# Attention stack on one core: projection weights, Wo and the key cache read already transposed

## What is computed

```python
q = einsum('bsd,ed->bse', x, Wq)   # 32 heads of 128
k = einsum('bsd,ed->bse', x, Wk)   # 8 heads of 128
v = einsum('bsd,ed->bse', x, Wv)   # 8 heads of 128
q, k = rope(rmsnorm(q, q_norm_w)), rope(rmsnorm(k, k_norm_w))
k_all = concat(k_cache[block_table], k)   # 512 cached keys + 32 new ones
v_all = concat(v_cache[block_table], v)
probs = softmax(where(valid, q @ k_all.T * scale, -1e30))
out = x + einsum('bse,de->bsd', probs @ v_all, Wo)
```

## Time and profile before

| | |
|---|---|
| median of 3 runs | 1507.56 us (1506.31 to 1509.15) |
| span of the profiled execution | 1508.6 us |
| TensorE busy | 1439.5 us, 95% |
| VectorE busy | 979.2 us, 65% |
| ScalarE busy | 813.0 us, 54% |
| GpSimd busy | 736.6 us, 49% |
| layers, projection, attention, output begin at about | 0, 203, 558, 1300 us |
| DMA | 275 MB, 182 GB/s over the span |

### The profile page before, as it was taken

How to read it: one execution, slowest core, us unless ns; L and a number is a source line. 1 busy time by engine, 2 the same in 40 slices (tenths; PEclk the granted TensorE clock), 3 DMA queues, 4 the chain that set the end, 5 groups by cost and what they waited for, 6 DMA issues and landing times. The chain is left out here.

```text
span 1508.6 us, 32191 instructions
## 1 busy us (share of the span) xinstructions
PE 1439.5 (95%) x9308; PEld 1265.8 (84%) x9308; DVE 979.2 (65%) x2630; ACT 813.0 (54%) x1930; POOL 736.6 (49%) x738
## 2 busy tenths in 40 slices
PE   5988989999999958999999999999999999789999
PEld 4766879999999947999999999998999999678887
DVE  4669966666666547777777777777777777542221
ACT  2156734444444336777777777776777777431111
POOL 2004027787777766665656666664656665000000
PEclk9999999999999978999999999999999999899999
DMA  6310034555554579988888888897988885443332
GB/s 187 135 50 18 22 127 112 171 143 170 170 170 136 162 216 277 250 239 241 257 244 235 251 249 238 244 253 202 258 234 243 259 238 152 144 156 122 124 117 76
DMA packets 273737, 275.13 MB, mean 182 GB/s; under 512 B 61461, under 2 KB 231701, under 8 KB 273686
## 3 DMA queue, kind: packets, MB, share of 16 engines
q1 hardware_dynamic: 263638, 249.24, 57.1%
q0 software_dynamic: 9472, 25.21, 6.2%
q10 hardware_dynamic: 576, 0.05, 0.0%
HBM read 219.88 MB, written 54.53 MB: 182 GB/s over the span
## 5 line engine op out<-in xcount | busy, mean ns | idle before, releaser
L1212 DVE CUSTOM_DVE_ANT_1 att_neg<-att_mask,att_ps 128x576 f32<-128x576 f32 x256 | 193.0, 754 | 154.8 <-PE att_ps L95 154.8
L1105 POOL TENSOR_TENSOR att_k_lo<-att_kT,att_k_hi 128x544 fp32r<-128x544 f32 x128 | 173.4, 1355 | 143.2 <-ACT att_k_hi L1314 143.2
L1105 POOL TENSOR_TENSOR att_k_lo<-all_room_a,att_k_hi 128x544 fp32r<-128x544 f32 x128 | 174.2, 1362 | 136.4 <-ACT att_k_hi L1314 136.4
L1299 ACT ACTIVATE att_prob<-att_neg,att_nmax 128x544 f32<-128x544 f32 x256 | 191.6, 748 | 29.0 <-DVE att_nmax L1212 6.3
L1305 ACT ACTIVATE att_pT<-att_pb 128x256 f32<-128x256 f32 x256 | 98.1, 383 | 183.7 <-PE att_pb L1145 183.7
L93 PE MATMUL att_ps<-att_k_hi,att_q_lo 128*128 128x288 f32 (+1 forms) x512 | 171.3, 335 | 12.0 <-POOL att_k_lo L1105 11.9
L93 PE MATMUL prj_ps<-prj_wt_hi,early_xT_lo 128*128 128x512 f32 (+1 forms) x512 | 178.4, 349 | 2.2 <-DVE prj_wt_lo L892 2.2
L94 PE MATMUL prj_ps<-prj_wt_lo,early_xT_hi 128*128 128x512 f32 (+1 forms) x512 | 173.5, 339 | 0.0
L95 PE MATMUL prj_ps<-prj_wt_hi,early_xT_hi 128*128 128x512 f32 (+1 forms) x512 | 172.9, 338 | 0.0
L94 PE MATMUL att_ps<-att_k_lo,att_q_hi 128*128 128x288 f32 (+1 forms) x512 | 148.9, 291 | 0.0
L95 PE MATMUL att_ps<-att_k_hi,att_q_hi 128*128 128x288 f32 (+1 forms) x512 | 148.9, 291 | 0.0
(11 more groups left out here) (169 smaller groups left out, 3860.9 us busy)
## 6 DMA issues: line engine op xcount, KB each, us to landing
all_room_a<-kt_scratch SPq DMA_DIRECT2D x256, 128.0 KB, 3.7
att_kT<-kt_scratch SPq DMA_DIRECT2D x256, 128.0 KB, 3.4
all_room_b<-in_L_cond_v_cache SPq DMA_DIRECT2D x160, 128.0 KB, 3.0
att_vc<-in_L_cond_v_cache SPq DMA_DIRECT2D x160, 128.0 KB, 3.1
q_scratch<-prj_qst SPq DMA_DIRECT2D x64, 256.0 KB, 2.2
o_scratch<-att_ost SPq DMA_DIRECT2D x32, 512.0 KB, 4.5
out_o_n<-o_scratch SPq DMA_DIRECT2D x32, 512.0 KB, 3.4
all_room_b<-in_L_cond_v_cache POOLq DMA_DIRECT2D x96, 128.0 KB, 3.9
```

The lines of the kernel that those rows point to most:

```text
L1105: g.tensor_tensor(k_lo[j % SPLITS][:], kT[j // HK % 2][:, :, j % HK, :], f32(k_hi[j % SPLITS][:]), ALU.subtract).then_inc(k_split, 1)
L1212: v.tensor_tensor_reduce(halves[0], halves[1], ps[j % 2][:, :, 0:KA], 1.0, 3.0e38, ALU.add, ALU.min, nmax[j % 2][:]).then_inc(maxed, 1)
L1299: act.activation(prob[j % 2][:], neg[j % 2][:, 0:KEYS], ACT.Exp, bias=nmax[j % 2][:, 0:1], scale=-1.0, accum_out=total[j % 2][:]).then_inc ...
```

## The change

The host now hands over three arrays in another layout (`laid_out`): `wqkv_t`, for each key head the rows 0 to 511 by its 768 columns of Wq, Wk and Wv; `wo_t`, Wo transposed; `k_cache_t`, each page as [128, 8 heads, 32 positions]. The kernel drops all transposes of weights, of Wo and of the key cache, the `pw` banks, the stores to and the existence of `kt_d`, and the loads of `kn`. The hi and lo splits read the loaded weights from SBUF. In the projection they are now four pieces per head, 768 columns each, in bodies t = 0, 2, 4, 6; TensorE has a new wait ahead of `multiply(j + 2)` at t = TT - 2 = 6. `load_head` is one DMA in place of three. In the output stage two chunks (1024 columns) are split at once, and SP's waits ahead of a slice's load are on the splits.

```diff
-def load_head(eng, inp, c, tile, sem):
-
-    for name, rows, o in zip(("L3_cond_Wq", "L3_cond_Wk", "L3_cond_Wv"), (QW, D, D), (0, REP, REP + 1)):
-        src = inp[name].rearrange("(c o p) i -> c p o i", p=P, o=rows // P)[bass.ds(c, 1)]
-        eng.dma_start(tile[:, o:o + rows // P, :], src.rearrange("a p o i -> (a p) o i")).then_inc(sem, 16)
...
+def load_head(eng, inp, c, tile, sem):
+
+    src = inp["wqkv_t"][bass.ds(c, 1)].rearrange("a (k p) e -> p (a k) e", p=P)
+    eng.dma_start(tile, src).then_inc(sem, 16)
...
+        def split_at(t, last_head):
+
+            return t % 2 == 0 and not last_head
...
                     if t == 0 and not tail:
 
-                        sp.wait_ge(job_t, job_of(c, 0))
-                        load_w(c + 2, slot)
+                        sp.wait_ge(w_hi_done, (c + 1) * KC)
+                        sp.wait_ge(w_lo_done, (c + 1) * KC)
+                        load_head(sp, inp, c + 2, wn[slot][:], w_in[slot])
...
-                pe.wait_ge(w_in[0], 48)
-                for g in range(WJ):
-                    weight_job(g, 0, first_banks[g])
-                pe.wait_ge(job_dve, WJ)
+                pe.wait_ge(w_lo_done, KC)
                 multiply(0)
                 multiply(1)
...
-                        if t == 0 and not last_head:
-                            pe.wait_ge(w_in[1 - slot], (it + 1 + slot) * 48)
-                        if not cache_step(t, last_head):
-                            weight_job(t, 1 - slot, pw[:, t % 2])
-                        else:
-                            pe.wait_ge(kn_in[t % 2], (c + 1) * 16)
-                            cache_job(t % 2)
                     if not (tail and j >= UNROLL - 2):
 
                         pe.wait_ge(roped, n + 1)
                         pe.wait_ge(v_staged, n + 1)
+                        if t == TT - 2:
+                            pe.wait_ge(w_lo_done, (c + 2) * KC)
                         multiply(j + 2)
...
+                    if split_at(t, tail and slot == 1):
+                        if t == 0:
+                            act.wait_ge(w_in[1 - slot], (it + 1 + slot) * 16)
+                        k = t // 2
+                        act.activation(wt_hi[1 - slot][:, k, :], wn[1 - slot][:, k, :], ACT.Copy).then_inc(w_hi_done, 1)
...
+                def split_lo(k, slot, done):
+
+                    dve.wait_ge(w_hi_done, done)
+                    v.tensor_tensor(wt_lo[slot][:, k, :], wn[slot][:, k, :], f32(wt_hi[slot][:, k, :]),
+                                    ALU.subtract).then_inc(w_lo_done, 1)
...
+                    if split_at(t, tail and slot == 1):
+                        k = t // 2
+                        split_lo(k, 1 - slot, (c + 1) * KC + k + 1)
                     if not (tail and j >= UNROLL - 2):
                         rope(j + 2, n + 2)
...
-    eng.dma_start(tile[:], inp["L3_cond_Wo"][:, s * w:(s + 1) * w].rearrange("(o p) e -> p o e", p=P)).then_inc(sem, 16)
+    eng.dma_start(tile[:], inp["wo_t"][s * w:(s + 1) * w].rearrange("(c p) o -> p c o", p=P)).then_inc(sem, 16)
...
                 for s in range(2, SL):
-                    sp.wait_ge(w_turned, (s - 1) * CS)
+                    sp.wait_ge(w_hi, (s - 1) * CS // WG)
+                    sp.wait_ge(w_lo, (s - 1) * CS // WG)
...
-                turn(0)
                 for i in range(UNROLL):
-                    if i + 1 < Q:
-                        turn(i + 1)
                     body(0, i, False)
...
-                    for c in range(q * CQ, (q + 1) * CQ):
-                        act.wait_ge(w_turned, c + 1)
-                        act.activation(wt_hi[:, c, :], pw[c % 4][:], ACT.Copy).then_inc(w_hi, 1)
+                    for c in range(q * CQ, (q + 1) * CQ, WG):
+                        s = c // CS
+                        act.wait_ge(w_in[s % 2], 16 * (s // 2 + 1))
+                        act.activation(wt_hi[:, c:c + WG, :], wn[s % 2][:, c % CS:c % CS + WG, :], ACT.Copy).then_inc(w_hi, 1)
...
-                    for c in range(q * CQ, (q + 1) * CQ):
-                        dve.wait_ge(w_hi, c + 1)
-                        v.tensor_tensor(wt_lo[:, c, :], pw[c % 4][:], f32(wt_hi[:, c, :]), ALU.subtract).then_inc(w_lo, 1)
+                    for c in range(q * CQ, (q + 1) * CQ, WG):
+                        s = c // CS
+                        dve.wait_ge(w_hi, c // WG + 1)
+                        v.tensor_tensor(wt_lo[:, c:c + WG, :], wn[s % 2][:, c % CS:c % CS + WG, :],
+                                        f32(wt_hi[:, c:c + WG, :]), ALU.subtract).then_inc(w_lo, 1)
```

More of the change, by code:

```diff
@@ L645, in stage_project @@
         pt = m.psum("pt", [P, 2 * BANK])
-        pw = m.psum("pw", [P, 2, BANK])
-        first_banks = [pw[:, 0], pw[:, 1]] + [x[:, i * BANK:(i + 1) * BANK] for x in (pt, ps[1]) for i in range(2)]
         w_in = [w_in0, m.sem("w_in1")]
[L651 to L654, removed]
+        w_hi_done = m.sem("w_hi_done")
+        w_lo_done = m.sem("w_lo_done")
         mm_done = m.sem("mm_done")
@@ L1037, in load_keys @@
             for j, page in enumerate(pages):
[L1038 removed]
+                load_key_page(eng, inp, kT[slot], j, page, kq_in[slot])
         def load_new_values(eng, b, slot):
@@ L1366, in stage_output @@
         x3, y = ([room[:, (2 * a + i) * H:(2 * a + i + 1) * H] for i in range(2)] for a in range(2))
-        pw = [m.psum(f"pw{i}", [P, BANK]) for i in range(4)]
         py = [m.psum(f"py{i}", [P, BANK]) for i in range(2)]
-        w_turned = m.sem("w_turned")
         w_hi = m.sem("w_hi")
@@ L1427, in _ @@
             def _(pe):
-                def turn(q):
-                    for c in range(q * CQ, (q + 1) * CQ):
-                        s = c // CS
-                        if c % CS == 0:
-                            pe.wait_ge(w_in[s % 2], 16 * (s // 2 + 1))
-                        if c >= 4:
-                            pe.wait_ge(w_lo, c - 3)
-                        for o in range(KC):
-                            t = pe.transpose(pw[c % 4][:, o * P:(o + 1) * P], wn[s % 2][:, o, c % CS * P:(c % CS + 1) * P],
-                                             ident[:])
-                        t.then_inc(w_turned, 1)
                 def body(it, i, tail):
@@ L1573, in inverse_frequencies, with laid_out @@
     return (np.float32(1.0) / np.power(np.float32(THETA), np.arange(0, D, 2, dtype=np.float32) / np.float32(D))).astype(np.float32)
+def laid_out(inputs):
+    a = {n: np.asarray(inputs[n]) for n in INPUTS}
+    heads = lambda n: a[n].reshape(HK, -1, H)
+    rows = np.concatenate([heads("L3_cond_Wq"), heads("L3_cond_Wk"), heads("L3_cond_Wv")], axis=1)
+    for n in ("L3_cond_Wq", "L3_cond_Wk", "L3_cond_Wv"):
+        del a[n]
+    a["wqkv_t"] = rows.transpose(0, 2, 1)
+    a["wo_t"] = a.pop("L3_cond_Wo").T
+    a["k_cache_t"] = a.pop("L3_cond_k_cache").transpose(0, 3, 2, 1)
+    a["rope_inv_freq"] = inverse_frequencies()
+    return {n: np.ascontiguousarray(x) for n, x in a.items()}
 def kernel(**inputs):
@@ L1581 @@
     arrays, args = {}, {}
-    for name in INPUTS + ["rope_inv_freq"]:
-        a = inverse_frequencies() if name == "rope_inv_freq" else np.ascontiguousarray(inputs[name])
+    for name, a in laid_out(inputs).items():
         arrays[f"in_{name}"] = a
```

122 lines of the change are left out of this document (23 added, 99 removed).

## The result

| | before | after |
|---|---|---|
| median of 4 runs | 1506.96 us (1506.31 to 1509.15) | 1519.52 us (1515.15 to 1521.20) |
| span of the profiled execution | 1508.6 us | 1513.5 us |
| TensorE busy | 1439.5 us | 1406.3 us |
| GpSimd busy | 736.6 us | 754.9 us |
| DMA | 275 MB | 258 MB |

The ratio of the times is 1.0078, with a 95% interval of 1.0061 to 1.0095: the change makes the kernel slower, by 12.6 us between the medians and 11.8 by the ratio. All ratios leave out one run that took 3484 us, of the kernel with the key cache's part alone. The forecast was 6.0 slower, 1513.6; the range of 1499 to 1526 holds the time. TensorE is busy 33 us less and the kernel is later all the same, so the loss is idle time and a low clock (a matmul's record is also longer while the clock is low, so part of that loss stands in the busy time).

A forecast was written before the change was run, and what follows sets the result against it. TensorE was taken to bound the projection, attention and the end of the output stage. Removed jobs -30.3, stalls +29.6, clock +11.2, start -0.4 and output -4.1 gave +6.0, so 1513.6 us, range 1499 to 1526.

The forecast's parts named there:

- The ruler: Projection: distances between five-transpose groups (L822) price removed work at 16.4 us for weight jobs and 13.9 for cache jobs.
- The estimate of 123 us: Projection: 448 removed transposes at about 275 ns each; the prediction used the steps' 30.3 us instead.
- The stall: Projection, body 6: TensorE waits for the last lo piece until S + 4.8, S starting body 5's transposes; 4.2 us, seven heads, 29.6.
- VectorE held by GpSimd: Last lo subtraction in the projection waits for GpSimd's addition (L946); stall 4.2 us with this, 3.3 without.
- the three earlier pieces: Projection, bodies 0, 2, 4: each delays GpSimd by about 0.9 us, costed at zero; up to 10 us without cover.
- The clock: Projection: granted clock falls after each of seven stalls, costing 1.6 us each, 11.2 us; bounds zero and 23 us.
- rival (b): Projection stalls: clock stays low twice as long, as at 1041; 11.8 us more, 1525 us; chance 0.10.
- The start: Start of the projection: first splits take 4.6 us in place of 5.0 before TensorE's first matmul, a gain of 0.4.
- The output stage: Output stage: unit 2 starts 5.5 us earlier, less 1.5 for low clock; a gain of 4, bounds 0 and 7.
- Attention: Attention keeps its instructions and reads key pages from another tensor in the same pieces; effect put at zero.
- The sum: Whole kernel: -30.3 + 29.6 + 11.2 - 0.4 - 4.1 = +6.0 us, added to the median for 1513.6 us.
- rival (f): Projection: no stall, for instance because pieces are ready earlier; the change gives its full 34.8 us, 1472.8; chance 0.04.

## Why the prediction held, and where it was off

**The ruler: right.** Reading the cost of a job from the distance of the L822 groups gave 16.4 and 13.9 us; the runs have 16.2 and 14.0. The estimate of 123 us from the Trainium skill's figure for one transpose ("TensorE: Matmul & The Clock Gate", section "Part 4: PE-mode transpose") is refuted. The skill states that figure for bf16, and the record here has 272 ns in float32; but the transposes of weights and cache in the loop were worth 30.2 us, and the output stage as a whole 4.9.

**The stall: right, in size and in its parts.** Laid out was S + 4.8, measured is S + 4.67; 4.2 us a head, 29.6 in all, against 29.6 by the steps with the clock up. That the tenths agree is luck: the layout itself gives 4.26 a head, the rounded 4.2 gives 29.4. VectorE held by GpSimd costs 0.84 us of it, against 0.9. The Trainium skill, "SBUF — State Buffer", section "SBUF: two separate sides", calls it an exclusive lock held for the whole instruction; the trace agrees, with 0.95 us for the subtraction alone and 1.78 beside GpSimd's addition. Putting the three earlier pieces at zero was right too: no step up to body 61 but the seven is longer than 4.77 us.

**The clock: right that it falls, wrong in size.** This is the term that was mis-sized: "Matmul work in 3.4 us at half speed loses 1.7, less if part of the low stretch falls in the idle time. I take 1.6 us each." Measured are 2.1 a head by the kernel with work in the stall, 14.4 to 14.9 in all against 11.2. In the trace of after the low stretch lasts 6.8 us at five of the seven stalls, where it begins 1.2 to 1.9 us before TensorE does, and 3.4 at two, where it begins 1.3 us behind it. So 5.0 to 5.6 us of it lie on matmuls in five heads and 3.4 in two, and the steps are 2.2 to 2.6 and 1.6 us longer than the 8.99 with the clock up: the 1.6 was right for the short stretch, and the caveat on the idle time was right, but most stretches are the long one. The row that showed this length was there, 6.6 us at 0.52 behind 1041.45; it went into rival (b) as a case for all seven heads, in place of a mixture. One row can't give its share: behind the same idle time of 2.15 us in attention the ten traces of this case have a low stretch of 6.8 us five times, of 3.4 three times, of 10.2 once, and none once.

**The start: right.** The first multiply comes at 207.22 in place of 208.41, 1.2 us earlier, but 0.7 of that is the end of the first three layers, 199.86 in place of 200.56, which the change doesn't touch. From there to the first multiply TensorE takes 7.36 us in place of 7.85: 0.5, where 0.4 was forecast.

**The output stage: right in the trace.** Unit 2 starts 34.9 us behind SP's first issue (1310.46), where 36 had been laid out, and the stage is 4.9 us shorter against 4.1 in the sum (whose own terms, 1341.95 - 1336.6 less 1.5, give 3.9). Over all traces the stage takes 207.1 to 208.6 us as changed (without the earlier load of `o_n`) and 211.1 to 212.2 as it was in the kernel before, so 4.9 is near the upper end. Alone it shows as 2.3 us by the ratio, with 4.1 inside the interval.

**Attention: zero, as far as can be told.** It was put at zero because its instructions don't change. TensorE's busy time in it hardly changes, 730.4 and 728.3 us, yet from body 61 to its end the trace of after is 3.1 us shorter. The low stretches in that part last 30.7 us together in before and 23.9 in after; 6.8 us less at half speed is 3.4. The same instructions take 748.6 to 754.2 us in the seven traces with the changed projection and 752.8 to 753.3 in the three without it: a kernel gets its low stretches at other places from trace to trace, and a difference of a few us between two single traces can come from that alone. The same holds between runs: those of after have a mean clock of 0.967, 0.965, 0.963 and 0.961, and take 1515.15, 1518.47, 1520.57 and 1521.20 us.

**The sum.** +6.0 became +12.6. The clock term is 3.2 to 3.7 of the difference of 6.6. The rest is in the part without a stall: it was summed to a gain of 34.8, 1472.8 in rival (f), and the kernel with the last piece one body earlier has 1476.85, a gain of 30.1 between the medians and of 31.8 by its ratio. The removed jobs are not what is missing there (30.2 of 30.3), and neither is the start (22.3 us from the end of the first three layers to body 0, in place of 22.5). The trace of that kernel is 30.8 us shorter than that of before: the loop 30.2 and the output stage 3.5 shorter, the first three layers 2.2 and attention 1.0 longer. With the pieces in bodies 0 to 3 the span is 33.8 shorter, though the times are the same. The parts alone show the same in their times, 2.3 for 4.1 and 12.5 for 13.9, each inside its interval. So some 3 to 5 us of the 34.8 don't show; that they go in low stretches elsewhere is likely by the spread of the traces, but no run shows it.

## What to carry to other kernels

Work that leaves the bounding engine pays only if what replaces it is ready before it is wanted: here 30 us of removed transposes were outweighed by seven waits of 4.2 us and their clock, and moving one piece by one body turned +12.6 into -30. When a producer and its consumer stand in the same body, lay out that body against the consumer's start, with every engine's queue in it, and look for a VectorE instruction with two SBUF inputs beside one of GpSimd, which took turns here. An idle time of a few us on TensorE should be priced with the matmuls behind it at the lower clock; here that was half the stall's length on top. Compare stages over several traces before a few us are put down to the change: the same instructions moved by up to 5.6 us.

## What the runs showed of the hardware

The stall of 4 us costs 2.1 more by the clock, and sixteen matmuls of 512 columns in it keep the granted clock at 1.00 (2.4 GHz) through it, with a gain of 14.4 us over seven stalls. At the projection's start, 20 of them bring body 0 2.4 us nearer to the end of the first three layers (20.0 us in place of 22.4). In front of units 1 and 2 of the output they bring nothing in the end, since these wait for the slices of Wo.

Holding goes both ways and takes no account of size: GpSimd's step on 128 x 5 elements takes 0.91 us in place of 0.20 when it meets the rest of VectorE's subtraction. It costs an engine with slack nothing: the 28 pieces hold GpSimd up for 20 us in all, spread out or in four bodies in a row, and no step of TensorE gets longer by it.
